# One sorted buffer of 136 tiles for the last stage of a four-layer network, in place of two of 72

## What is computed

```python
logits = flat @ router_w.T
probs = softmax(logits)
topk_probs, topk_idx = top_k(probs, 2)
topk_probs = topk_probs / (sum(topk_probs) + 1e-09)
gates = sum over k of topk_probs[:, k] * one_hot(topk_idx[:, k], 8)
h = silu(flat @ w1[e].T) * (flat @ w3[e].T)      # for each expert e
out = sum over e of gates[:, e] * (h @ w2[e].T)
```

## Time and profile before

| | |
|---|---|
| time, median of 3 runs | 1226.98 us (1225.48 to 1228.63) |
| the profiled execution's own time | 1228.42 us |
| its span, first to last instruction | 1226.7 us |
| mean granted TensorE clock | 0.952 |
| busy: PE, DVE, ACT, POOL | 1048.8, 587.0, 524.9, 502.7 us |
| the 144 slot tiles, first to last multiply on DVE | 812.6 to 1200.5 us |

### The profile page before, as it was taken

The page is one execution under the profiler, slowest core; times in us unless marked ns, Lnnn a source line. Parts: engine busy times, 40 slices in busy tenths (PEclk is TensorE's granted clock), DMA queues, the critical chain, the costliest instruction groups (busy, mean ns, idle before and its releaser), DMA issues.

```text
span 1226.7 us, 17966 instructions
## 1 busy us (share of the span) xinstructions
PE 1048.8 (85%) x5576; PEld 737.6 (60%) x5577; DVE 587.0 (48%) x1719; ACT 524.9 (43%) x980; POOL 502.7 (41%) x799
## 2 busy tenths in 40 slices
PE   4779966889998899998998989987779988988991
PEld 2334322567666544644873455467779888888891
DVE  7855873211064265555746634353273333333454
ACT  5567844234232476653357645544222222222220
POOL 5922265630633320000310366525336666565651
PEclk9799988999999999999999989999799999999996
DMA  9930001232322100000000111163255757668766
GB/s 278 365 154 1 1 33 63 78 93 69 94 78 78 29 18 0 1 1 0 1 1 1 64 43 45 38 179 112 78 180 187 242 167 258 189 225 312 239 199 226
DMA packets 100884, 135.53 MB, mean 110 GB/s; under 512 B 12434, under 2 KB 69570, under 8 KB 99906
## 3 DMA queue, kind: packets, MB, share of 16 engines
q1 hardware_dynamic: 88002, 108.00, 27.6%
q0 software_dynamic: 12800, 26.50, 6.6%
HBM read 88.81 MB, written 45.65 MB: 110 GB/s over the span
## 4 chain that ended last, share of the span: by engine, by line
PE 63%; DVE 14%; issue 8%; another core or an unknown queue 7%; ACT 5%; POOL 2%; DMA 1%; DVEq 0%; ACTq 0%; POOLq 0%; SPq 0%
PE bank L1263 14%; PE bank L1289 12%; PE bank L1270 9%; PE bank L1299 7%; PE bank L1148 4%; PE bank L1028 4%; PE bank L1183 2%; DVE sb_R L1945 2%; PE bank L1211 2%; PE bank L1200 1%; PE bank L994 1%; PE bank L1172 1%; DVE sb_R L1430 1%; PE bank L1192 1%
## 5 line engine op out<-in xcount | busy, mean ns | idle before, releaser
L1263 PE MATMUL bank<-sb_R,sb_wih_sb 128*128 128x512 f32 (+2 forms) x504 | 202.9, 553 | 12.5 <-ACT sb_R L879 6.6
L1945 DVE TENSOR_TENSOR sb_R<-sb_R,bank 114x384 f32<-114x384 f32 x144 | 79.6, 553 | 230.8 <-PE bank L1299 138.2
L879 ACT ACTIVATE sb_R<-bank,sb_lb_sb 128x512 f32<-128x512 f32 (+2 forms) x252 | 151.0, 633 | 88.6 <-PE bank L1270 78.4
L650 POOL DMA_INDIRECT expert_out<-sb_R,sb_slot_row x144 | 140.8, 977 | 111.3 <-DVE sb_R L1903 36.3
L913 ACT ACTIVATE sb_R<-bank 114x384 f32<-114x384 f32 x144 | 69.4, 490 | 250.0 <-PE bank L1289 123.4
L1263 PEld LDWEIGHTS bank<-sb_R,sb_wih_sb 128*128 128x128 f32 x504 | 96.4, 193 | 111.7 <-issue 82.7
L1289 PE MATMUL bank<-sb_xt,sb_BIG 128*114 128x128 f32 x864 | 111.0, 280 | 19.6 <-DVE sb_R L1945 15.0
L1299 PE MATMUL bank<-sb_BIG,sb_R 114*128 x864 | 123.6, 279 | 2.1 <-issue 1.6
L1289 PEld LDWEIGHTS bank<-sb_xt,sb_BIG 128*114 128x114 f32 x864 | 102.2, 183 | 23.9 <-issue 23.0
L644 POOL DMA_INDIRECT sb_R<-sorted_out,sb_dest_i x64 | 60.8, 950 | 125.7 <-DMA sorted_out<-sb_R 44.0
L1299 PEld LDWEIGHTS bank<-sb_BIG,sb_R 114*128 114x128 f32 x864 | 110.0, 194 | 2.5 <-issue 2.3
(11 more groups left out here) (279 smaller groups left out, 1691.5 us busy)
## 6 DMA issues: line engine op xcount, KB each, us to landing
sb_BIG<-up_t SPq DMA_DIRECT2D x72, 342.0 KB
sb_wih_sb<-up_t SPq DMA_DIRECT2D x36, 342.0 KB
sb_whh_sb<-up_t SPq DMA_DIRECT2D x36, 342.0 KB
sb_XS<-expert_in SPq DMA_DIRECT2D x18, 528.0 KB
expert_in<-sb_R SPq DMA_DIRECT2D x18, 512.0 KB, 6.0
sb_R<-expert_out SPq DMA_DIRECT2D x7, 1024.0 KB, 6.7
sorted_in<-sb_R SPq DMA_DIRECT2D x9, 512.0 KB, 5.5
sb_XS<-sorted_in SPq DMA_DIRECT2D x18, 256.0 KB
```

The lines of the kernel that those rows point to most:

```text
L650: pool.indirect_dma_start(out=expert_out, out_offset=bass.IndirectOffsetOnAxis(ap=slot_row[:, i:i + 1], axis=0), in_=yd[i // 8 % RING][:, ...
L879: act.activation(gb[s][k][:, 0:c], bank[4 * s + k][:, 0:c], funcs[k], bias=lb_sb[:, (p - 1) * GATES + k:(p - 1) * GATES + k + 1]).then_inc ...
L1263: mm = pe.matmul(bank[4 * s + k][:, 0:c].rearrange("p (w b) -> p w b", b=GH), wih_sb[:, p - 1, k * P:(k + 1) * P], xin, start=True, stop=( ...
L1945: dve.tensor_tensor(hm[j % 2][0:HC, :], sl[j % 2][0:HC, :], bank[3 + 2 * (j % 2)][0:HC, 0:KU * P], ALU.mult).then_inc(d2_m, 1)
```

## The change

- One buffer `expert_in` of `NS` = 136 slot tiles for both halves: 128 *closed* tiles (`CLOSED1`), which are filled to the last row or are the last, and 8 *open* tiles, one for each expert, at slots 128 to 135. What an expert has left over from a batch of tokens goes into its open tile and the next batch goes on filling it. 136 tiles are computed, in 17 groups instead of 18.
- Tokens come in three batches: the first half (32 tiles), then two of 16 tiles. The groups run in the order 0 to 9, then 16 (the open tiles), then 10 to 15 (`GROUPS`). Group 7 is loaded when batch 1 has been scattered, and the eleventh group (the open one) when batch 2 has (`READY` = 7, 10).
- The second half's side work is laid out anew: `t_transposes` and `t_add` at slot tiles 0, 1, 2, 4, 6, 7, 8, 10; the layer norm in two parts of 16 tiles in place of four of 8; `r_norm` in part on DVE; the router product at tiles 12 to 15 and at 22, 24, 25, 26; the routing of batch 1 in 15 steps in tiles 16 to 30, that of batch 2 in 14 steps in tiles 30 to 43.
- POOL scatters batch 1 from slot tile 28 and batch 2 from 52, sends rows home before, between and after, and the last 107 from tile 72 on.
- The adds of the end come one at a time, at every second tile of the last 16, in place of two together in each of the last four groups.

The diff, cut to its core:

```diff
-    NSLOT1 = -(-(2 * NH + E - 1) // 8) * 8
+    CLOSED1 = 2 * NTILE
+    NS = CLOSED1 + E
+    BATCHES = ((0, NH), (NH, NH + NH // 2), (NH + NH // 2, NTILE))
+    READY = ((2 * NH - E + 1) // 8, (3 * NH - 2 * (E - 1)) // 8)
+    GROUPS = list(range(READY[1])) + [CLOSED1 // 8] + list(range(READY[1], CLOSED1 // 8))
...
-        T_TILES, RANK_TILE = 18, 21
-        Y_FIRST, IN_TILE, Y_TILE = 22, 26, 66
-        ND2 = HALVES * NSLOT1 // 8
-        D3_LOAD = ND2 - 5
+        T_AT = {1: 1, 2: 2, 4: 3, 6: 4, 7: 5, 8: 6, 10: 7}
+        XN_ACT_AT = {9: 0, 11: 2, 17: 4, 19: 5, 21: 6, 23: 7}
+        XN_DVE_AT = {9: 1, 11: 3}
+        R_AT = {12: 0, 13: 1, 14: 2, 15: 3, 22: 4, 24: 5, 25: 6, 26: 7}
+        ROUTE_AT = {1: 16, 2: 30}
+        HOME_FIRST, LN_AT, IN_AT, HOME_MORE, HOME_REST = 24, (2, 7), (28, 52), 29, 72
+        ND2 = NS // 8
+        HALF_GROUPS = (READY[1] + 1, ND2)
+        D3_LOAD = ND2 - 3
+        D3_ADD = 8 * (ND2 - 2)
...
             for g in range(1, ND2):
-                if g + 1 < ND2 and g + 1 != D2H:
+                if g + 1 < ND2 and g + 1 not in READY:
                     d2_load(g + 1)
+                if g == READY[0]:
+                    sp.wait_ge(rd.tiles, 2)
+                elif g == READY[1]:
+                    sp.wait_ge(rd.tiles, 3)
                 d2_weights(g)
-                if g + 1 == D2H:
-                    sp.wait_ge(s_scat[1][1], 32 * NH)
+                if g + 1 in READY:
+                    sp.wait_ge(s_scat[1][1 + READY.index(g + 1)], 16 * NH)
                     d2_load(g + 1)
...
+            for i in range(HOME_FIRST):
+                if i in LN_AT:
+                    t_finish(1, LN_AT.index(i), NGH // 2)
+                rows_home(i)
+            rows_in(1)
+            for i in range(HOME_FIRST, HOME_MORE):
+                rows_home(i)
+            rows_in(2)
+            for i in range(HOME_MORE, 8 * ND2):
+                pool.wait_ge(d2_h, min(HOME_REST + 5 * (i - HOME_MORE) // 8, 8 * ND2))
+                rows_home(i)
...
+                for b, at in ROUTE_AT.items():
+                    if i == at + 2:
+                        route_exp(1, rd, b)
+                    if i == at + 5:
+                        route_copies(1, rd, b)
...
+                if i in R_AT:
+                    r = R_AT[i]
+                    if r == 0:
+                        pe.wait_ge(t_x, 2 * NGH)
+                    elif r == NGH // 2:
+                        pe.wait_ge(rd.ranks_sb, 2)
+                    else:
+                        pe.wait_ge(rd.st, NGH + r)
+                    r_transposes(1, r, bank[1])
...
+            def d2_route(p, step):
+                if step == 0:
+                    p.scores()
+                    p.keys(0)
+                elif step == 1:
+                    p.chosen(0)
+                    p.second()
+                elif step == 2:
+                    p.keys(1)
+                elif step == 3:
+                    p.chosen(1)
+                elif step in (4, 5, 6):
+                    p.weights(step - 4)
+                elif step in (7, 8, 9):
+                    p.counts(step - 7)
+                elif step == 10:
+                    p.places()
+                elif step in (11, 12):
+                    p.rows(step - 11)
+                elif step == 13:
+                    p.table()
+                elif step == 14 and p.b == 1:
+                    p.carries()
...
-                    if j == 2 and 0 <= g - (ND2 - NF) < NF:
-                        d3_add(g - (ND2 - NF))
+                    if D3_ADD <= i < D3_ADD + 4 * NF and i % 2 == 0:
+                        d3_add((i - D3_ADD) // 4, (i - D3_ADD) // 2 % 2)
```

More of the change, by code:

```diff
@@ L88, in build @@
         sorted_out = nc.dram_tensor("sorted_out", [NSLOT0 * P, D], F32, kind="Internal").ap()
-        expert_in = [nc.dram_tensor(f"expert_in{h}", [NSLOT1 * P, DR], F32, kind="Internal").ap() for h in range(HALVES)]
-        PADS = HALVES * NSLOT1 * P
+        expert_in = nc.dram_tensor("expert_in", [NS * P, DR], F32, kind="Internal").ap()
+        PADS = NS * P
         expert_out = nc.dram_tensor("expert_out", [PADS + 2 * TOK, D], F32, kind="Internal").ap()
@@ L444, in _ @@
             sp.wait_ge(w_in, W_ALL)
-            for rows in [sorted_in] + expert_in:
+            for rows in (sorted_in, expert_in):
                 zv = rows.rearrange("(p n) d -> p (n d)", p=P)
@@ L616, in scatter @@
                     pool.wait_ge(zeroed, ZEROS)
-                rows, src = (sorted_in, XN[:, half * NH:(half + 1) * NH, :]) if layer == 0 else (expert_in[half], XR)
+                rows, src = (sorted_in, XN[:, half * NH:(half + 1) * NH, :]) if layer == 0 else (expert_in, XR)
                 for t in range(half * NH, (half + 1) * NH):
@@ L1029, in hidden, with rank @@
                               start=True, stop=True).then_inc(r.h, 1)
-            def rank(layer, r, half):
-                m = flat(space[layer, half].mask)
-                pe.wait_ge(r.mask, half + 1)
-                pe.matmul(bank[1][:, 0:EH], before[:, :], m, start=True, stop=True)
-                pe.matmul(bank[1][:, EH:2 * EH], ones[:, :], m, start=True, stop=True).then_inc(r.ranks, 1)
+            def rank(layer, r, b):
+                m = flat(space[layer, b].mask)
+                n = m.shape[1]
+                pe.wait_ge(r.mask, b + 1)
+                pe.matmul(bank[1][:, 0:n], before[:, :], m, start=True, stop=True)
+                pe.matmul(bank[1][:, n:2 * n], ones[:, :], m, start=True, stop=True).then_inc(r.ranks, 1)
             def b1_transposes(b):
@@ L1508, in t_stats, with r_norm @@
                 ins.then_inc(t_ln, 1)
[L1510 to L1511 removed]
+            def r_norm(half, g, done):
+                if half == 0:
+                    dve.wait_ge(t_rstd, g // 2 + 1)
+                else:
+                    dve.wait_ge(t_rstd, NGH // 2 + 1 + g // (NGH // 2))
+                    dve.wait_ge(s_scat[1][0], 32 * NH)
                 for t in range(4 * g, 4 * g + 4):
@@ L1577, in weights @@
                     ex = by_token(w.exps)
-                    den, p1, e1, p2 = (wts[:, i, :] for i in range(4))
+                    den, p1, e1, p2 = (self.wt(i) for i in range(4))
+                    meta = self.rows_in
                     if part == 0:
-                        dve.wait_ge(self.r.flat, 2 * self.half + 2)
+                        dve.wait_ge(self.r.flat, 2 * self.b + 2)
                         L(dve.tensor_reduce(den, ex, AX_X, ALU.add))
@@ L1880, in _ @@
                         in_d[0].chosen(1)
-                    if half > 0 and n in (8, 9):
-                        in_d[0].weights(n - 8)
+                    if half > 0 and n == 8:
+                        in_d[0].weights(0)
+                    if half > 0 and n == 9:
+                        in_d[0].weights(1)
+                        in_d[0].weights(2)
                     if half > 0 and n == 10:
-                        in_d[0].counts()
+                        for part in range(3):
+                            in_d[0].counts(part)
                     if half > 0 and n == 11:
@@ L1982, in _ @@
             for i in D3_OF[1]:
-                d3_add(i)
+                for k in range(2):
+                    d3_add(i, k)
 def layouts(i):
```

441 lines of the change are left out of this document (248 added, 193 removed).

## The result

The changed kernel takes 1215.65 us (median, 1207.77 to 1225.74) against 1223.97 for the kernel before in the same session (1220.31 to 1233.58): a ratio of 0.9927, 95% interval 0.9903 to 0.9951, so 8 to 9 us faster. The forecast was 1203 us, that is nearly 24 us less than before. The direction was right; the gain is little more than a third of it.

A forecast was written before the change was run, and what follows sets the result against it. Bound: a chain of waits, PE alone near the end (1.98 us a tile), DVE while it routes. 19.9 + 7 - 4.5 - 1 + 2.5 = 23.9 us off 1228.4: 1204.5, or 1203 against the median; range 1190 to 1218.

The forecast's parts named there:

- Part 4: Edges: LSTM stage's batch 0 bookkeeping loses 1 us (ends 0 and 3); the adds of the end gain 2.5.
- Part 1: Eight slot tiles fewer in the plain stretch, at 2.49 us each: 19.9 us gained, bounds 17 and 23.
- the adds: Adds of the end one at a time, not two together, fit under the tile pace: 2.5 us gained, ends 0 and 4.
- tail: The 26.2 us behind the last tile stay, as its reads, adds and stores are unchanged: 0 us.
- the gates: SP's two waits for a scatter before loads: no cost unless POOL is over some 4 us late.
- Part 3: Routing in two batches, some 40 us on DVE in place of 20: 4.5 us lost, ends 0 and 12.
- Part 2: Graph work and router, first 18 tiles: 7 us gained (ends 0 and 14); router blocks cost 10.8 wherever put.
- rival 2: Front gains nothing, routing costs its full 12 us, adds give 0: 7 us off, 1220 (band 1211 to 1223); chance 0.18.
- the 11.27 us of the earlier trace: Wait before tile 13's multiply in the kernel before, put down to an unknown queue; whether it returns was left unsettled.

The follow-up runs named there:

- b_again: The kernel before, unedited, profiled once more in a session of the faster pace: 1138.91 us.
- a_again: The changed kernel, unedited, profiled once more in a session of the faster pace: 1126.53 us, 0.989 of the kernel before.
- after: First profile of the changed kernel, at the slower pace: the profiled execution took 1212.6 us, the median of the runs is 1215.65.
- a_ref: The changed kernel unaltered, timed again as a base in a slower session: 1213.93 us, 0.9925 of the kernel before.
- a_ref2: The changed kernel unaltered, as a base in another slower session: 1218.67 us, 0.99 of the kernel before.
- a_home: Changed kernel with GpSimd's order moved: third batch's rows in from tile 48, not 52, remaining rows home from 68, not 72; 0.9881 of the kernel before.
- a_order3: Changed kernel, rank multiplications, copies and third batch's routing one tile later, last four router tiles at 24 to 27; 0.9843 of the kernel before, faster session.
- a_spread: Changed kernel with new routing order, earlier sends, third batch's table in two tiles, routers on every second tile; 1111.23 us, 0.9758 of the kernel before, faster session.
- a_order: Same edit as a_order3 on the changed kernel, in a slower session: 0.9859 of the kernel before, median 6.7 us under a_ref.
- a_silent2: Changed kernel with GpSimd sending only the first 29 tiles home, other 107 sends left out; second run, faster pace: 0.9808 of the kernel before.
- a_noload: Changed kernel without loading expert weights from the eighth group on (values wrong), faster pace: 0.9882 of the kernel before.
- b_thrice: The kernel before, unedited, profiled yet again at the faster pace; tiles 0 to 17 took 59.2 us.
- b_less8: The kernel before without its last eight slot tiles (136), nothing else of the change: 1125.71 us, 0.9879 of the kernel before.
- a_all3: Changed kernel with the edits of a_home and a_order3 and the third batch's table made in two tiles: 0.985 of the kernel before.

## Why the prediction fell short

The second column is the faster sessions (b_again to a_again), the third the three profiles of the changed kernel in slower sessions (after, a_ref, a_ref2), as a mean, against the one of before. The cut is at tile 60, behind the last effect of the third batch's table.

| term | predicted | faster | slower |
|---|---|---|---|
| start of the stage (Part 4, LSTM) | -1 | +0.8 | -4.9 |
| tiles 0 to 59 (Parts 2 and 3: +7 - 4.5) | +2.5 | -5.5 | -2.5 |
| tile 60 to the last (Part 1, and the adds: 19.9 + 2.5) | +22.4 | +19.1 | +21.4 |
| tail | 0 | -1.9 | -1.7 |
| sum | 23.9 | 12.5 | 12.3 |

**The tail.** "The 26.2 us behind the last tile stay: five blocks to read, ten adds, five stores, none of them changed" failed. None of those is changed, but what they wait for is: GpSimd's last send. The prediction checked that its sends of the scatter are in time for the gates, which was right in the faster sessions (TensorE doesn't stand behind either gate), and did not ask whether it still catches up by the end. Its own rule for the sends, 138 tiles of 136 for the last one, would have told. a_home undoes it, and the last send with it, so this is shown.

**Part 3.** This is the step that failed most. The prediction has this part losing 4.5 us: 4.5 for steps of VectorE that are too long for a tile, 1.5 for the second exponential and 2 for the copy at tile 22, less 3.6 that the kernel before lost too. Two of its items came out in the faster session: the wait for the copy, 1.8 us, and the one for the third batch's table, 2.3 us where 2.8 were put down. But it looked at one hand-over, tile 22, and not at each for who is queued behind it: the wait of 2.1 us for the mask at tile 20 was not in it, nor what follows once TensorE has lost its lead. a_order3, which changes nothing but the order, takes the whole excess of the change over the kernel before away (153.0 against 153.2 for tiles 0 to 59), so in the faster sessions these two places in the order are worth the 5.5 us that the change loses here. In the slower ones the same edit is worth 9.4 and 11.4 us on these tiles, and brings them 5.5 and 6.6 under the kernel before, near the +7 of Part 2. The widths, and with them 40 us of VectorE's routing in place of 20, were right: tiles 0 to 44 show 84.5 us of VectorE against 66.5 (30.0 + 54.5 and 26.0 + 40.5). That this much costs little was right too: in a_order3 TensorE waits 2.3 us in all for VectorE's multiplies behind tile 18, 2.1 of them for the table.

**Part 2.** "A tile with a block of the router ... eight are 8 x 1.35 = 10.8 ... wherever they are put" failed. On every second tile they cost less. The cleanest comparison is tiles 10 to 17 in the faster sessions, which hold four router tiles in either version: 27.3 us in a row (a_order3), 23.6 on every second tile (a_spread), 16.7 at 2.09 a tile. That is 2.6 and 1.7 us for each router tile with all that lies beside it. In a row, each one's transposes wait 0.82 us for the logits of the one before, three times in a_order3 and not once in a_spread, and TensorE loses its lead. The 7 us for the wait was taken as half of what might come, and came out near by its size in the slower sessions: tiles 12 and 13 of before took 20.6 us there and 8.1 in the faster ones, tiles 13 and 14 of the changed kernel 13.6 to 14.8 and 9.1. So 12.5 us of such waiting became about 5. That this is the layout's doing isn't shown, since before has one profile at that pace. In the faster sessions there is no such wait to save, and the +7 is missing there.

**Part 1 and the adds.** Eight tiles fewer are worth eight tiles at the session's pace, as predicted: with the adds it is 19.1 and 21.4 of 22.4. The pace is 2.09 us where TensorE is busy without a gap, so 8 x 2.09 = 16.7 in the faster sessions, close to the lower bound of 17. From tile 60 on it is 2.42, 2.44 and 2.47 in the slower profiles against 2.47 before. The adds, one at a time, gave 0.8 and not 2.5. The step that failed is that a pair of adds, which makes a tile of VectorE's longer (3.12 us in b_again), makes the stage longer by as much: TensorE doesn't wait once from 1050 us to the last tile there, and the eight tiles around a pair take 16.9 us in place of 16.7. The other 1.7 us of the 19.1 are the reading of the home rows in SyncE's queue, ahead of the weights: the step it makes is 6.2 us in b_again and 4.5 in a_again.

**Part 4, LSTM.** Nothing is seen lost there: the changed kernel's 778.7 lies within the 777.8 to 779.5 of before. The -4.9 of the slower ones lies within the scatter of the start. **The gates** cost nothing in the faster sessions, as predicted. In the slower ones the step at tile 52 is 5.2, 5.1 and 4.3 us, 2.7 in the kernel before; no run tells what stands there.

The measured 1215.65 lies in the band of rival 2 (1211 to 1223), but rival 2 isn't what happened: front and routing together lost 5.5 us in the faster sessions and 2.5 in the slower ones, and not 12. Only its last item, nothing from the adds, nearly came true. The result is the forecast's mechanism with three stretches priced too well. In the faster sessions it is 8.0 us on tiles 0 to 59, 3.3 on the rest and 1.9 in the tail, against 1.8 the other way at the start, where profiles of one kernel differ by 1.7. In the slower sessions, the ones that were forecast, it is 5.0, 1.0 and 1.7, and 3.9 at the start.

What stays open is the slower pace itself, and with it how far the first session's 8.3 us are the change's own. The 8.3 us between the medians of the first session, with 11.5 in both later ones and 12.4 at the faster pace, isn't split further.

## What to carry to other kernels

An engine that is not the bottleneck can still set the end: when the number of tiles changes, work out by the written rule of each other queue when its last item is let go, and compare it with the last tile. Where steps are laid out by tile number, look at each cross-engine hand-over and leave one whole tile between maker and user; two hand-overs in adjacent tiles cost 5.6 us here at the faster pace, while of 18 us more of VectorE's work only one step, the table's 5.4 us in one tile, made TensorE wait, 2.3 us. And price a term with the pace of more than one session, or give its bound from the engine's own work.

## What the runs showed of the hardware

The same code has two paces. In the faster sessions a plain tile is 2.09 us with TensorE busy throughout. In the slower ones about half of the plain tiles take over 2.6 us: from tile 60 on it is 38 of 75 in after, up to 4.8 us each, and 1 of 75 in a_again, at a granted clock of 0.99 in both. Some of these steps, the long ones in the front above all, stand at the same tiles from one execution to the next. VectorE's multiply of tile 14, in after, a_ref and a_order (in this order), all at the slower pace:

```profile
860.88 0.56 DVE L2090 TENSOR_TENSOR sb_R<-sb_R,bank 114x384 f32<-114x384 f32 x1 [6.17 <-remote]
```
```profile
856.15 0.56 DVE L2090 TENSOR_TENSOR sb_R<-sb_R,bank 114x384 f32<-114x384 f32 x1 [6.14 <-remote]
```
```profile
854.51 0.55 DVE L2090 TENSOR_TENSOR sb_R<-sb_R,bank 114x384 f32<-114x384 f32 x1 [6.11 <-remote]
```

In a_again the same wait is 3.72 us. What the multiply needs there is TensorE's down product and ScalarE's silu; in after the last record of the product ends at 858.3, 2.6 us before the multiply starts, and the profile names nothing that ends the wait. At tile 30 the step to the next multiply is 7.6, 8.9 and 7.9 us in these three and 3.2 in a_again. A wait that recurs to 0.1 us at one place belongs to that place of the program and not to chance. So a wait like the 11.27 us of the earlier trace rows has to be priced as one that can come back; whether that one does in the kernel before isn't shown. Which resource it is, no run here shows: a_silent2 and a_noload would have told GpSimd's sends and the weights apart from it, and both came at the faster pace. The Trainium skill, Runtime: NRT & Kernel Launch, section Instruction fetch mechanics, has an engine's instructions fetched in blocks of 256 by its own DMA queue, the cost of crossing into the next block mostly hidden. Blocks would agree with the fixed places; a hidden cost would not if this is what stands there. The traces don't show a slow fetch at tile 14: the nearest packet of the instruction queue starts at 852.4 in after and at 809.9 in a_again, takes 0.93 us in both, and none moves from 853.5 until the multiply starts. Whether an engine stands for another reason at such a place isn't shown.

The other is the read of the home rows: 4 MB in SyncE's queue ahead of the weights, with GpSimd's sends beside them, make TensorE stand for 2.3 to 6.25 us at the faster pace (a_again 2.3, b_thrice 2.5, b_less8 6.25). At the slower pace the chain of a_all3 holds this, the load of a tile's weights, behind four reads of home rows that were issued at 1116.9 to 1118.2:

```profile
1122.63 11.00 DMA sb_BIG<-up_t
```

TensorE still had work for most of it and stood 1.9 us.
